# Expert layers of a graph transformer block: the first layer is issued one unit ahead, between the second layer's tiles

## The reference, cut to what matters

```python
hh = jax.nn.gelu(x @ W1[ei] + b1[ei], approximate=False)     # 256 -> 512
out = out + g[..., None] * (hh @ W2[ei] + b2[ei])            # 512 -> 256
```

## Time and profile before

| | us |
|---|---|
| median of three runs | 2258.68 (2253.89 to 2258.86) |
| profiled execution, span | 2712.5 |
| profiled execution, its own time | not given beside its span |
| POOL's first to last gather, L857 | 102.8 to 1387.9 |
| POOL's first to last gather, L1821 | 1503.8 to 2453.3 |
| PE's expert work | 1511.4 to 2464 |

### The profile page before, as it was taken

One profiled execution on the slowest core, in us unless ns is written; L12 is line 12 of the kernel. 1 busy time (PEld: TensorE's weight loads), 2 busy tenths in 40 slices (PEclk: granted clock), 3 DMA queues, 4 the chain that ended last, 5 costly groups with the idle time before them and its releaser, 6 DMA issues. The chain is left out here.

```text
span 2712.5 us, 26680 instructions
## 1 busy us (share of the span) xinstructions
PE 1935.5 (71%) x7528; PEld 1334.5 (49%) x7528; DVE 1195.4 (44%) x2204; ACT 893.4 (33%) x1910; POOL 1474.4 (54%) x1512
## 2 busy tenths in 40 slices
PE   5588778876766776666547788878888788884235
PEld 4454445454544544444336455555555565553223
DVE  6353222344454555443348433324424344256368
ACT  3433345444435343443315211321222213132124
POOL 2456456565656665556630566666666666661510
PEclk8888789887888888777775799998999889897555
DMA  5443222234334433435329511121211212215544
GB/s 182 147 132 123 62 82 86 72 117 135 117 112 130 130 118 105 131 93 179 89 61 296 208 36 50 36 70 36 70 36 50 56 45 61 51 36 172 159 148 152
DMA packets 197044, 282.80 MB, mean 104 GB/s; under 512 B 43024, under 2 KB 147443, under 8 KB 195762
## 3 DMA queue, kind: packets, MB, share of 16 engines
q0 software_dynamic: 61280, 115.13, 15.9%
q1 hardware_dynamic: 97218, 121.11, 13.5%
q10 hardware_dynamic: 38416, 44.96, 5.0%
HBM read 195.29 MB, written 85.80 MB: 104 GB/s over the span
## 5 line engine op out<-in xcount | busy, mean ns | idle before, releaser
L857 POOL DMA_INDIRECT ag_msg<-xn_tab,step_src x784 | 782.1, 998 | 504.9 <-issue 224.0
L1821 POOL DMA_INDIRECT edge_rows<-hx_d,gat_src x648 | 621.2, 959 | 329.6 <-issue 187.4
L1125 PE MATMUL ag_ps<-ag_msg,ag_hot 128*128 x1760 | 494.0, 430 | 113.5 <-issue 67.8
L1125 PEld LDWEIGHTS ag_ps<-ag_msg,ag_hot 128*128 128x128 f32 x1760 | 366.8, 216 | 238.5 <-issue 181.2
L879 DVE TENSOR_TENSOR acc<-acc,ag_ps 128x257 f32 x440 | 186.0, 423 | 671.1 <-remote 329.8
L2011 PE MATMUL ex_psY<-co_rows 128*128 128x256 f32 x1568 | 401.4, 413 | 100.2 <-issue 44.5
L2011 PEld LDWEIGHTS ex_psY<-co_rows 128*128 128x128 f32 x1568 | 320.8, 208 | 175.6 <-issue 68.7
L1996 PE MATMUL ex_psF<-co_rows 128*128 128x448 f32 x896 | 360.7, 557 | 42.8 <-ACT co_rows L2061 16.9
L1301 ACT ACTIVATE gat_self<-iota_row,step_nloc 128x128 f32<-128x128 f32 x880 | 271.4, 388 | 343.3 <-issue 199.1
L1935 DVE TENSOR_TENSOR hi_one_low<-hi_numbers,hi_low 128x2048 bf16<-128x2048 f32 x64 | 146.4, 2287 | 481.3 <-remote 309.5
L1996 PEld LDWEIGHTS ex_psF<-co_rows 128*128 128x128 f32 x896 | 172.2, 196 | 214.5 <-issue 187.6
(11 more groups left out here) (377 smaller groups left out, 2004.9 us busy)
## 6 DMA issues: line engine op xcount, KB each, us to landing
y_d<-co_rows ACTq DMA_DIRECT2D x28, 896.0 KB
co_rows<-y_d SPq DMA_DIRECT2D x28, 896.0 KB, 9.5
ag_msg<-xn_tab,step_src POOLq DMA_INDIRECT x784
xnT<-base_d SPq DMA_DIRECT2D x7, 1792.0 KB
edge_rows<-hx_d,gat_src POOLq DMA_INDIRECT x648
base_d<-xnT ACTq DMA_DIRECT2D x7, 1024.0 KB
sums_d<-edge_rows SPq DMA_DIRECT2D x5, 1344.0 KB
xg<-in_x_dram SPq DMA_DIRECT2D x7, 896.0 KB, 6.1
```

The lines of the kernel that those rows point to most:

```text
L857: pool.indirect_dma_start(msg[:, q, u, 0:D], None, c.xn_tab, bass.IndirectOffsetOnAxis(ap=t.idx[:, at:at + 1], axis=0)).then_inc(s_g[q], 16)
L1125: last = nc.tensor.matmul(bank[(at + r) % BANKS][:, 0:ROWW], hot[:, k, u0 + r * JOIN + j, :], ring[:, j * ROWW:SLOTS * ROWW][:, ds(places[ ...
L1821: pool.indirect_dma_start(G[:, j % RING, w, :], None, c.hx_d, bass.IndirectOffsetOnAxis(ap=plan.idx[:, at + w:at + w + 1], axis=0)).then_i ...
```

## The change

PE's order becomes a list. Pass n holds the fills of unit n and the tiles of unit n-1 in turn (fill, tile, fill, tile, ...); pass 0 has fills alone, pass 1 has its tiles first and then its fills, and pass 28 tiles alone. `hh` and `yo` have two buffers each, with a store semaphore for each `yo`. `yT` is loaded in two halves, each when the last fill that reads it is done. The histogram's products no longer stand in batches of 16: those of a pass are spread evenly over its steps. Pass 0 gets 32 of them, 4 after each fill; passes 1 to 5 get 32 or 48, 2 to 4 after each step; passes 9 to 11, 14 to 16, 19 to 21 and 24 to 26 get 64, 4 or 5 after each step. That makes 263 places. ACT and POOL follow the same list. To make room, `low`, `high` and `past` move into buffers that are free then, and some semaphores are joined.

```diff
     due = (7, 12, 17, 22, 27)
-    halves = [(0, 12)] + [(2 * n + 3, 2 * n + 9) for n in due[:4]]
+    beside = [(0, 6)] + [(n + 2, n + 5) for n in due[:4]]
...
-        past = sb("gs_past", [P, GT, P])
+        past = xs[:].rearrange("p a h w -> p (a h w)").rearrange("p (t n) -> p t n", t=GT)
...
-        hh = lent[1][:, at:at + HC * GN].rearrange("p (k a b) -> p k a b", k=HC, a=2)
+        hidden = [lent[1][:, at:at + HC * GN], sb("ex_hidden", [P, HC * GN])[:]]
+        hh = [x.rearrange("p (k n) -> p k n", k=HC) for x in hidden]
         at += HC * GN
-        yo = lent[1][:, at:at + GT * D].rearrange("p (t d) -> p t d", t=GT)
+        yo = lent[1][:, at:at + 2 * GT * D].rearrange("p (b t d) -> p b t d", b=2, t=GT)
...
+        def passes(n):
+
+            fills = [(0, n, i) for i in range(NF)] if n < UNITS else []
+            tiles = [(1, n - 1, u) for u in range(NS)] if n else []
+            if n == 1:
+                return tiles + fills
+            return [x for pair in itertools.zip_longest(fills, tiles) for x in pair if x]
+
+        order = [x for n in range(UNITS + 1) for x in passes(n)]
...
                 def turned(g):
-                    sp.wait_ge(s_f, g * EXPERTS * NF)
-                    sp.dma_start(yT, c.x2nT_d[:, :, g * GN:(g + 1) * GN]).then_inc(s_yT, 16)
+                    for i in range(2):
+
+                        sp.wait_ge(s_f, g * EXPERTS * NF - HC * (1 - i))
+                        turned_half(g, i)
...
                 def paced(k):
 
-                    n, u = divmod(k * GROUPS * EXPERTS * EXPERT_UNITS // W_LOW - LEAD, EXPERT_UNITS)
-                    if n >= 0 and u < NF:
+                    at = k * len(order) // W_LOW - LEAD
+                    if at < 0:
+                        return
+                    layer, n, u = order[at]
+                    if layer == 0:
                         pool.wait_ge(s_f, n * NF + u + 1)
-                    elif n >= 0:
-                        pool.wait_ge(s_s, n * NS + u - NF + 2)
+                    else:
+                        pool.wait_ge(s_s, n * NS + u + 2)
...
+                def hist(at):
+
+                    k, i = divmod(at, HIST)
+                    if i == 0:
+                        pe.wait_ge(s_one, k + 1)
+                    last = nc.tensor.matmul(psC[:, 0:HIGHS], one_low[:, k % 2, i, :], one_high[:, k % 2, i, :],
+                                            start=(at == 0), stop=(at == LANE - 1))
+                    if i == HIST - 1:
+                        last.then_inc(s_hist, 1)
+
+                def counted(n):
+
+                    return HIST * sum((min(max(n, h0), h1) - h0) * (k1 - k0) // (h1 - h0) for (k0, k1), (h0, h1) in zip(asked, beside))
+
+                for n in range(UNITS + 1):
+                    both = passes(n)
+                    c0, c1 = counted(n), counted(n + 1)
+                    for q, (layer, unit, u) in enumerate(both):
+                        if layer == 0:
+                            first(unit, u)
+                        else:
+                            second(unit, u)
+                        for at in range(c0 + (c1 - c0) * q // len(both), c0 + (c1 - c0) * (q + 1) // len(both)):
+                            hist(at)
...
+                for n in range(UNITS + 1):
                     if n in due:
                         exponentials(due.index(n))
-                    expert(n // EXPERTS, n % EXPERTS)
+                    for layer, unit, u in passes(n):
+                        if layer == 0:
+                            gelu(unit, u)
+                        elif u % 2 or u == NS - 1:
+                            copied(unit, u // 2)
+                        if layer == 1 and u == NS - 1:
+                            stored(unit)
```

More of the change, by code:

```diff
@@ L1 @@
+import itertools
 from contextlib import ExitStack
@@ L1701, in gat_gather_experts @@
         spare = hot[:].rearrange("p t l -> p (t l)")
[L1702 to L1705, removed]
+        high, hdst, low_i, far, away, low = (spare[:, i * LANE:(i + 1) * LANE] for i in range(6))
+        hsrc, hdst, low_i = (x.bitcast(I32) for x in (high, hdst, low_i))
         one_low = sb("hi_one_low", [P, 2, HIST, P], BF16)
@@ L1713, in gat_gather_experts @@
         s_blank, s_blankst = c.sem("gg_blank"), c.sem("gg_blankst")
[L1714 to L1715 removed]
+        s_hin, s_one, s_hist, s_hot = (c.sem("hi_" + n) for n in ("in", "one", "hist", "hot"))
         sums_v = c.sums_d.rearrange("(p w) r -> p w r", p=P)
@@ L1782, in _ @@
                 sp.wait_ge(s_s, GROUPS * EXPERTS * NS + 1)
-                sp.wait_ge(s_yst, 16 * GROUPS * EXPERTS)
+                for i in range(2):
+                    sp.wait_ge(s_yst[i], 16 * (UNITS // 2))
                 for g in range(len(early)):
@@ L1989, in _ @@
                 pe.sem_inc(s_s, 1)
[L1991 to L2027, removed]
-                        for i, layer in enumerate((first, second)):
-                            layer(g, e)
-                            n = 2 * (g * EXPERTS + e) + i
-                            for (k0, k1), (h0, h1) in zip(asked, halves):
-                                if h0 <= n < h1:
-                                    for k in range(k0 + (n - h0) * (k1 - k0) // (h1 - h0), k0 + (n - h0 + 1) * (k1 - k0) // (h1 - h0)):
-                                        hist(k)
+                def first(n, i):
+                    g, e = divmod(n, EXPERTS)
+                    if e == 0 and i % HC == 0:
+                        pe.wait_ge(s_yT[i // HC], 16 * g + 16)
+                    if i == 0 and n < 2:
+                        pe.wait_ge(s_w[n], 32 * (EXPERTS - 1) if n else 48)
+                    pe.wait_ge(s_ge, n * NF + i + 1)
+                    for k in range(KC):
+                        last = nc.tensor.matmul(psF[i % FB][:, 0:HB], w1[:, e, k, (i % HC) * P:(i % HC + 1) * P],
+                                                yT[:, k, (i // HC) * HB:(i // HC + 1) * HB], start=(k == 0), stop=(k == KC - 1))
+                    last.then_inc(s_f, 1)
@@ new lines, in second @@
+                def second(n, u):
+                    e = n % EXPERTS
+                    f, half = divmod(u, 2)
+                    if u == 0:
+                        pe.wait_ge(s_ge, n * NF + HC + FB)
+                    elif u == WHOLE:
+                        pe.wait_ge(s_ge, n * NF + NF + FB)
+                    if half == 0:
+                        pe.wait_ge(s_yc, n * len(FILLS) + f + 1)
+                    for k in range(HC):
+                        last = nc.tensor.matmul(psY[f % YB][:, half * D:(half + 1) * D], hh[n % 2][:, k, u * P:(u + 1) * P],
+                                                w2[:, e, k, :], start=(k == 0), stop=(k == HC - 1))
+                    last.then_inc(s_s, 1)
```

71 lines of the change are left out of this document (38 added, 33 removed).

## The result

Twenty runs of each on one chip: before 2253.95 us, after 2259.62. The ratio is 1.0024, 95% interval [1.0013, 1.0035]: slower by 5.4 us [2.9, 7.9], just under the 0.3% by which I told a difference from none. Of the 7.4 us between my 2267.0 and the 2259.62, 4.7 are the base: I had added my +8.5 to a median of three runs, 2258.68, and the median of twenty is 2253.95. The ratios in this document leave out executions over 1.5% above the fastest of the same kernel: beside f0 to f3 one of the 34 of the kernel before (3120.88 us) and one of nine in f1 (2794.60), and on the chip of e0 to e3, where the times scatter by some 2%, 9 of 28 of the kernel before and 6 of the 12 of e1.

A forecast was written before the change was run, and what follows sets the result against it. The prediction took POOL's chain of gathers to bound both gather stretches in timed runs. All terms were 0 us except the start's +8.5, taking the median from 2258.7 to 2267 us; range 2240 to 2282, the forecast's own 2262 to 2275.

The forecast's parts named there:

- the 454 us: Whole kernel: profile 2712.5 us against median 2258.68, read as waits that timed runs hardly have.
- The split: POOL's two gather stretches: 306 us of waits at L857 and 141 us at L1821, absent in timed runs.
- my freed sum: Profiled 2712.5 us less both stretches' waits gives 2265.5, within 7 us of the median.
- The stall: Start of the stage: PE stands 10.5 us behind fill 0 for DVE's tables; gather 14 goes 8 us late.
- the start's term: First histogram product behind fill 0 makes every later gather 8 to 9 us late: +8.5 us, bounds +4 to +16.
- `yT` in halves: Loads of `yT`: same bytes, 7 more SP transfers of about 0.6 us each, priced at 0 us.
- Waits for ACT: PE at the two layers: nearly all 71 us go in a profile, 10 in a timed run, hidden under POOL.
- Places of the products: Histogram products between PE's steps: 0.066 us per place, 15.0 us more on PE, 0 in the sum.
- Rival 1: PE's waits for ACT are real in timed runs too: -43 us, 2215; half real, 2251; chance 17%.
- Rival 2: The loss at the start is absorbed by later POOL waits or faster gathers: 0 us, 2258; chance 23%.
- Rival 3: PE is the bound, with gathers well under 1.25 us in timed runs: +18 us, 2277; chance 10%.
- The sharpest test: Next profile's span may be shorter by some 30 us while the median is longer.

The follow-up runs named there:

- f0: The kernel before, unchanged, on a second chip: 2258.72 us.
- f3: The kernel before with its first histogram batch behind fill 0 instead of fill 7, on the second chip: ratio to the kernel before 1.0027.
- f1: The changed kernel, unchanged, on the second chip: ratio to the kernel before 1.0040, +9.0 us.
- e0: The kernel before, unchanged, profiled again on the chip where it is slow: 2674.01 us.
- e3: The changed kernel without POOL's waits for PE, on the slow chip: 3220 us, ratio to the kernel before 1.209.
- e1: The changed kernel with first histogram batch behind fill 7, rest of passes 0 and 1 from pass 1's fourth step, slow chip: ratio to before 0.9947.
- i0: The changed kernel with late first products (batch 0 behind fill 7) and group 0's rows in one load: ratio to the kernel before 0.9997.
- h2: The changed kernel with the rows of group 0 in one load instead of two halves, fourth chip: ratio to the kernel before 1.0021.
- f2: The changed kernel with first histogram batch behind fill 7, rest of passes 0 and 1 from pass 1's fourth step, second chip: ratio to before 0.9984.
- g1: The changed kernel with POOL's waits looking 15 fills and tiles back instead of 7, third chip: ratio to the kernel before 0.9999.

## Why the prediction came out as it did

**What bounds the kernel: right, by a wrong story.** POOL's gathers bound the stage in the timed runs: from f1 to i0 only what lengthened them, a stall at gather 14, made the time longer. But I took the 454 us between the profile and the median for a difference between profiled and timed executions. e0 refutes it: the same kernel takes 2664 us unprofiled on another chip. That the profile of the earlier trace rows comes from such a chip is inferred: its clock (0.825, e0 has 0.827) and its waits are those of e0. The split was off too. f0 against the profile of the earlier trace rows is 258 us less before the first gather (I had 306), 116 less over the stage's gathers (I had 141), and 84 less in the tail, where I had counted nothing. That my freed sum met the median within 7 us was partly errors that cancelled. And the bound is shown for the changed stage alone. No run touched the gathers of L857, which take 1033.5 us in f0 where I had 979. A reading was off as well, without effect: the earlier trace rows has four busy slices, from 1721.75, not five from 1721.

**The stall: the mechanism right, the size not.** PE stands 10.8 us (forecast 10.5), and gather 14 waits for fill 2. I had 8 us for it; the changed kernel's profiles have 11.8, 10.0 and 11.8. I had gather 14 at 27.0 us behind the first, and it is 30.2, 28.3 and 30.2. **The step that failed is the size of the start's term, +8.5 us, and in its working two inputs.** The first is the tables: I took them to be done 21.2 us behind the first gather, as before. "`yT` in halves" was priced at 0 us, and SP's extra transfer, which "may make DVE's tables 0.6 us later", entered no sum. They are done at 23.6, 21.6 and 23.6. With one load in place of two (h2) they are at 21.1 again, and gather 14 goes at 26.7. The second is the clock at the restart: I took the lower level for about 4 us and 5.6 us from the first product to the end of fill 2. Measured are 5.3 to 5.5 and 6.3 to 6.4.

**The sum.** +8.5 us forecast; three measurements give +5.4 [2.9, 7.9], +9.0 [5.0, 13.1] and +10.6 [6.8, 14.4], 8.3 in the mean. So on the record's own measurement the term was too big by 3 us, while by the length of the stall it was too small by 2 to 3. The two inputs above explain the stall and not the time; that the mean of three comes out at the forecast is luck, two errors that cancel. Where the difference goes stays open. The gathers as a whole are 12.6, 5.8 and 9.4 us longer than in f0 for stalls of 11.8, 10.0 and 11.8, and what else they lose scatters by as much from one profile to the next. The absolute forecast, 2267, was off by 4.7 us more, since its base was a median of three runs.

**PE's part.** Waits for ACT: forecast 10 us gone in a timed run, measured 16.7 to 4.0. Places of the products: 263 of them, each with its 0.28 us in place of 0.22. From the first fill to the last product, without waits for ACT, PE took 729.8 us in f0 and 743.0 in f2, +13 where I had +15. All of it hidden, as said: g1 shows 9.6 us of later PE end at no cost. The Trainium skill, page "TensorE: Matmul & The Clock Gate", section "LDWEIGHTS (loading the stationary operand)", was the source of the open 62 ns for a place; f2 has 253 places, 217 more than f0, and 13 us over them is 61 ns. The trace agrees.

**The rivals.** Rival 1 (waits for ACT are real) is false where the kernel takes 2254 and partly true on the chip of 2664, where the waits are there in the profiles and are 41 us less in e1 than in e0. Whether they bring time there isn't shown, and the change as it is wasn't run on that chip. I set the Trainium skill's rule beside that rival ("Perfetto Trace Analysis", "Identifying Performance Opportunities": improve the most contended engine) and took PE for that engine by its busy products. The Trainium skill's same section says that for TensorE this share is not a good measure of how near it is to its roofline, and takes the FLOPs done and the share of its weight loads instead. By the weight loads, in the earlier trace rows, PE has 545 of 953 us and POOL 616, and in f0's gather stretch 523 and 625 of 833. Read so, the rule points at POOL, and the trace agrees: neither 13 us of PE's waits less (f0 to the changed kernel) nor 9.6 us of later PE end (g1) moved the time by what can be told. Rival 2 (absorbed) is false: three intervals exclude 1. Rival 3 (PE the bound) is false by g1, and its condition, gathers well under 1.25 us, is met in no profile. The sharpest test I named, a shorter profile beside a longer median, said nothing, since the length went with the chip and not with profiling (e0).

**What stays open:** why one chip takes 18% longer; whether the change as a whole gains there; what makes the load for the tables take up to 2 us longer with two loads in front of it; and why the three measurements of the changed kernel pay 5.4 to 10.6 us for stalls of 10.0 to 11.8.

## What to carry to other kernels

When a paced engine waits for positions in another engine's order, moving work to an early position moves those waits: look for the first wait whose position now stands behind something late, here one product behind fill 0. Where gathers bound, a late gather is paid for (5 to 11 us here for stalls of 10 to 12), while 11 us of idle PE cost nothing by themselves; so cost each stall by who waits for it. And an "equal bytes" change of a load need not be free at a stage's start: behind the split load, what the tables wait for came 0.5 to 2.5 us later. Before explaining a gap between a profile and the times, run the same kernel once more elsewhere.

## What the runs showed of the hardware

One of the four chips ran the same program in 2664 us where the others took about 2254, in profiled and timed runs alike. There alone PE was slowed beside gathers: one instruction per 1.40 us in the stretch of e3 shown, and the full pace in the pauses of the gathers and after the last. In e0, between the first and the last gather, 81 pairs of neighbouring instructions of PE (weight loads and products) start 0.70 us apart and 20 start 1.40 us apart, in f0 10 and none. With POOL's waits for PE taken out the change lost 21% there and 0.16% [-0.02, 0.33] on another chip. So the pacing, which brings nothing that can be told on an ordinary chip, is worth about 20% on that one. By the rows PE waited for nothing ("issue"); what in the chip does it is not shown.
